# Row-tiled, paired gram matmuls and 78-row turns in a recommendation tower on Trainium2

## The reference

```python
def _cin_layer(X0, Xi, W, b):
    Wr = W.reshape(H, F0_, Fi)
    return jnp.einsum('hjk,bjd,bkd->bhd', Wr, X0, Xi) + b[None, :, None]
e = jnp.stack([tbl_0[ids[:, 0]], ..., tbl_38[ids[:, 38]]], axis=1)      # (512, 39, 16)
X0 = e; Xi = X0; res = []
for W, b in ((W0, b0), (W1, b1), (W2, b2)):
    Xi = _cin_layer(X0, Xi, W, b)
    res.append(Xi.sum(axis=2))
h = jnp.concatenate([jnp.concatenate(res, axis=1), dense_ctx], axis=1)
h = jnp.maximum(h @ W_top1 + b_top1, 0.0)
h = jnp.maximum(h @ W_top2 + b_top2, 0.0)
y = h @ W_top3
```

## Time and profile before

| | |
|---|---|
| three runs | 655.06, 651.89, 655.04 us |
| median | 655.04 us |
| the profiled execution, its own time | 654.38 us |
| its span | 652.5 us |
| PE busy | 617.7 us (95%) |
| DVE busy | 581.6 us (89%) |
| ACT busy | 558.5 us (86%) |
| POOL busy | 470.9 us (72%) |
| TensorE clock | 1.00 of full speed |

### The profile page before, as it was taken

How to read it: one execution, slowest core, us unless ns; L and a number is a source line. 1 busy time by engine, 2 the same in 40 slices (tenths; PEclk the granted TensorE clock), 3 DMA queues, 4 the chain that set the end, 5 groups by cost and what they waited for, 6 DMA issues and landing times.

```text
span 652.5 us, 14351 instructions
## 1 busy us (share of the span) xinstructions
PE 617.7 (95%) x2595; PEld 477.3 (73%) x2595; DVE 581.6 (89%) x1233; ACT 558.5 (86%) x1767; POOL 470.9 (72%) x442
## 2 busy tenths in 40 slices
PE   0389999999999999999999999999999999999998
PEld 0146788787878787878788787878787878876673
DVE  0549999999999999999999999999999999999980
ACT  3048899999999999999899989999999999999782
POOL 6778898979797989989798979798987656420000
DMA  7533404131222314040414132231405050000200
GB/s 228 135 78 88 125 19 126 34 105 53 79 81 49 109 21 137 9 137 17 126 32 121 39 91 67 67 91 39 120 8 149 1 150 5 12 18 1 65 1 0
DMA packets 44274, 46.16 MB, mean 71 GB/s; under 512 B 20896, under 2 KB 27264, under 8 KB 44233
## 3 DMA queue, kind: packets, MB, share of 16 engines
q1 hardware_dynamic: 38482, 43.59, 23.0%
q0 software_dynamic: 5120, 1.32, 2.4%
q10 hardware_dynamic: 631, 0.74, 0.4%
HBM read 44.30 MB, written 1.31 MB: 70 GB/s over the span
## 4 chain that ended last, share of the span: by engine, by line
PE 88%; issue 4%; DVE 4%; POOL 1%; ACT 1%; DMA 1%; DVEq 0%
PE ya L528 12%; PE ya L530 12%; PE ya L529 12%; PE yd L528 9%; PE yd L530 8%; PE yd L529 8%; PE misc L511 5%; PE acc L500 4%; PE acc L499 3%; PE acc L501 3%; PE acc L504 2%; DVE chain L651 2%; POOL emb L390 1%; PE yd L611 1%; PE yd L609 1%
## 5 line engine op out<-in xcount | busy, mean ns | idle before, releaser
L779 ACT ACTIVATE prods<-ya,x0t 128x128 f32<-128x128 f32 x1472 | 452.0, 519 | 40.8 <-PE ya L530 37.8
L651 DVE SCALAR_TENSOR_TENSOR chain<-yd,x0t,chain 128x128 f32<-128x128 f32 x768 | 218.2, 343 | 4.9 <-remote 4.0
L390 POOL DMA_INDIRECT emb<-in_tables,rows x160 | 158.4, 990 | 35.4 <-issue 24.3
L528 PE MATMUL ya<-w1h,x1h 128*128 128x512 f32 (+1 forms) x384 | 166.4, 433 | 3.2 <-ACT prods L779 2.1
L437 POOL TENSOR_TENSOR prod0l<-prod,prod0h 120x512 fp32r<-120x512 f32 x98 | 127.6, 1302 | 47.8 <-ACT prod0h L788 47.2
L529 PE MATMUL ya<-w1l,x1h 128*128 128x512 f32 (+1 forms) x384 | 147.5, 384 | 0.0
L530 PE MATMUL ya<-w1h,x1l 128*128 128x512 f32 (+1 forms) x384 | 147.2, 383 | 0.0
L305 POOL TENSOR_TENSOR prod<-tiles,x0a 120x512 f32<-120x512 f32 x105 | 137.3, 1308 | 12.5 <-issue 4.2
L666 DVE TENSOR_REDUCE x2t<-prods 128x128 f32<-128x1792 f32 x64 | 129.2, 2019 | 2.4 <-issue 0.3
L666 DVE TENSOR_REDUCE prods<-prods 128x128 f32<-128x1536 f32 x64 | 111.7, 1746 | 0.1
L528 PE MATMUL yd<-w1h,x1h 128*128 128x512 f32 x256 | 102.5, 400 | 1.9 <-DVE prods L651 1.6
(11 more groups left out here) (102 smaller groups left out, 620.9 us busy)
## 6 DMA issues: line engine op xcount, KB each, us to landing
tiles<-x_rows SPq DMA_DIRECT2D x236, 78.0 KB
x0a<-x_rows SPq DMA_DIRECT2D x45, 80.0 KB
emb<-in_tables,rows POOLq DMA_INDIRECT x160
w<-in_w SPq DMA_DIRECT2D x3, 832.0 KB, 5.6
w<-in_w SPq DMA_DIRECT2D x13, 192.0 KB
tiles<-x_rows SPq DMA_DIRECT2D x32, 42.0 KB
x<-x_rows SPq DMA_DIRECT2D x16, 78.0 KB
x<-x_rows SPq DMA_DIRECT2D x16, 77.8 KB
```

Source lines behind the costliest of these rows:

```text
L390: pool.indirect_dma_start(emb[:, c % 2, fo * D:(fo + 1) * D], None, a["tables"], bass.IndirectOffsetOnAxis(ap=rows[:, c, fo:fo + 1].bitcas ...
L528: pe.matmul(out, x1h[:, c % 2, xs], w1h[:, cols], start=True, stop=False)
L651: dve.scalar_tensor_tensor(out, product, x, run if step else b1[:, :], ALU.mult, ALU.add).then_inc(yd_used, 1)
L779: mm = act.activation(prods[:, :, slot_of(q) + i], ya[(NA * g + k) % YA][:, i * H:(i + 1) * H], ACT.Copy, scale=turned(c)[:, g * F1 + j:g ...
```

## The change

- **Gram.** Each gram matmul becomes two, on rows 0 to 63 and rows 64 to 127 of the same operands, each with 160 columns and a bank of its own. They go out for two groups at once, after (0,6) and (2,6); ACT copies the two results after blocks 7 and 8. `diag` is half as wide and has four buffers. For the second bank one of ACT's four `ya` banks is given up (`YA` = 3).
- **Turn.** `x0` has two copies of the 39 rows; both halves of the turn have 78 rows. It now turns the next chunk, after (1,1), and not the one after next, after (3,1).
- **Layout of the data.** The columns of a chunk are ordered in two halves. `x0_rows` is stored by halves, so a transfer's pieces are 1 KB where they were 2 KB, and 64 bytes in the store where they were 128.
- **Rounding.** The first product of a chunk is rounded at (3,7), not (3,4).

```diff
-XB = 3
+XB = 2
-YA, YD = 4, 2
+YA, YD = 3, 2
+DIAGS = 4
-G_AFTER, TURN_1 = 6, (0, 8)
+G_AFTER, TURN_AFTER = 6, (1, 1)
-HIGH_AFTER = {0: (3, 4), 1: (0, 0), 2: (0, 5), 3: (1, 0), 4: (1, 5), 5: (2, 0), 6: (2, 5)}
+HIGH_AFTER = {0: (3, 7), 1: (0, 0), 2: (0, 5), 3: (1, 0), 4: (1, 5), 5: (2, 0), 6: (2, 5)}
...
-        scratch = nc.dram_tensor("x0_rows", (CHUNKS, FP, COLS), F32, kind="Internal").ap()
-        acc0, misc = ps("acc0"), ps("misc")
+        scratch = nc.dram_tensor("x0_rows", (CHUNKS, 2, FP, HCOLS), F32, kind="Internal").ap()
+        acc0, pair = ps("acc0"), ps("pair", (P, 2, 512))
+        misc = pair[:, 0, :]
...
-                pe.transpose(misc[:, XB * F:GROUPS * F], by_group[0:F, XB, :], const[0:F, C_ID:C_ID + F]
+                pe.transpose(misc[:, XB * F:2 * XB * F], by_group[:, XB, :], const[0:XB * F, C_ID:C_ID + XB * F]
                              ).then_inc(x0t_done, 1)
...
-            def gram_group(n, g):
-                pe.wait_ge(sums_done, 2 * n + 2)
-                pe.wait_ge(diag_ready, n + 1)
-                wait_done(pe, g_ready, n)
-                pe.matmul(misc[:, 0:GB * F1], x2t[:, g % 2, :],
-                          diag[:, g % 2, :, :].rearrange("p b j -> p (b j)"),
-                          start=True, stop=True).then_inc(g_done, 1)
+            def gram_groups(ns):
+                pe.wait_ge(sums_done, 2 * ns[-1] + 2)
+                pe.wait_ge(diag_ready, ns[-1] + 1)
+                wait_done(pe, g_ready, ns[0])
+                for i, n in enumerate(ns):
+                    for h in range(2):
+                        half, cols = slice(h * HROWS, (h + 1) * HROWS), slice(i * HB * F1, (i + 1) * HB * F1)
+                        mm = pe.matmul(pair[:, h, cols], x2t[half, n % 2, :],
+                                       diag[half, n % DIAGS, :, :].rearrange("p b j -> p (b j)"), start=True, stop=True)
+                mm.then_inc(g_done, len(ns))
...
-                        if q == G_AFTER + 1 and (g or prev):
-                            evacuate_gram(GROUPS * c + g - 1)
+                        if q == G_AFTER + 1 and (g == 2 or g == 0 and prev):
+                            evacuate_gram(GROUPS * c + g - 2, 0)
+                        if q == G_AFTER + 2 and (g == 2 or g == 0 and prev):
+                            evacuate_gram(GROUPS * c + g - 1, 1)
```

More of the change, by code:

```diff
@@ L38 @@
 GROUPS = CB // GB
+HB = GB // 2
+HROWS = P // 2
+HCOLS = COLS // 2
 R0 = F + 1
@@ L287, in load_x0a @@
             for u in range(3):
-                engine.dma_start(x0a[u * R0:(u + 1) * R0, :], chunk_rows(x)[0:R0, :]).then_inc(x0a_in, 16)
+                engine.dma_start(in_halves(x0a[u * R0:(u + 1) * R0, :]), chunk_rows(x)[0:R0]).then_inc(x0a_in, 16)
         def load_tile(engine, x, i):
@@ L293, in load_tile @@
             for row, a, b in segments(i):
-                engine.dma_start(tiles[a:b, i % L0_TILES, :],
-                                 chunk_rows(x)[row:row + b - a, :]).then_inc(tile_in[i % L0_TILES], 16)
+                engine.dma_start(in_halves(tiles[a:b, i % L0_TILES, :]),
+                                 chunk_rows(x)[row:row + b - a]).then_inc(tile_in[i % L0_TILES], 16)
         def multiply0(engine, x, i):
@@ L306, in multiply0 @@
                                  ALU.mult).then_inc(prod0_ready, 1)
-        hid, hid2 = (acc0, ya[0], ya[1], ya[2]), (yd[1], ya[3])
+        hid, hid2 = (acc0, ya[0], ya[1], ya[2]), (yd[1], pair[:, 1, :])
         block = ctx.enter_context(nc.Block())
@@ L316, in store_x0 @@
                 sp.wait_ge(x0_ready, x + 1)
[L317 to L320, removed]
+                by_row = scratch[x, :, :, :].rearrange("h (f o) n -> (h f) (o n)", f=FI)
+                for i, cols in enumerate((slice(0, FT * HCOLS), slice(FT * HCOLS, FO * HCOLS))):
+                    sp.dma_start(by_row[:, cols].rearrange("q (p b) -> p q b", b=CB // 2),
+                                 xt[0:(cols.stop - cols.start) // (CB // 2), i, :].rearrange("p (q b) -> p q b", b=CB // 2),
                                  ).then_inc(scratch_in, 16)
@@ L412, in sum_dims_last @@
                     pool.wait_ge(z_adds, {8: 1, 4: 2, 2: 3}[count])
[L413 removed]
+                out = z[:, (CHUNKS - 1) * CB:].rearrange("p (g b) -> p g b", g=2 * GROUPS)
                 pool.tensor_tensor(out, terms[:, :, 0, :], terms[:, :, 1, :], ALU.add).then_inc(z_sums, 1)
@@ L763, in evacuate_x1, with evacuate_gram @@
                                ACT.Copy).then_inc(x1h_ready, 1)
-            def evacuate_gram(n):
+            def evacuate_gram(n, i=0):
                 act.wait_ge(g_done, n + 1)
-                act.activation(gram[:, :, bass.ds(n * GB, GB)],
-                               misc[:, 0:GB * F1].rearrange("p (b j) -> p j b", b=GB),
+                cols = slice(i * HB * F1, (i + 1) * HB * F1)
+                act.activation(gram[:, :, bass.ds(n * GB, GB)].rearrange("p j (h b) -> p j h b", h=2),
+                               pair[:, :, cols].rearrange("p h (b j) -> p j h b", b=HB),
                                ACT.Copy).then_inc(g_ready, 1)
@@ L799, in chunk @@
                             evacuate_layout(c + 2)
-                        if lay and (g, q - 2) == turn_after(prev):
-                            evacuate_x0t(c + 2)
-                        if not prev and (g, q) == (TURN_1[0], TURN_1[1] + 1):
-                            evacuate_x0t(1)
+                        if nxt and (g, q - 2) == TURN_AFTER:
+                            evacuate_x0t(c + 1)
                         if not nxt and (g, q) == (1, 2):
@@ L808, in chunk @@
                             act.activation(dense, dense_raw, ACT.Copy).then_inc(dense_high, 1)
-                        if q == G_AFTER + 1 and (g or prev):
-                            evacuate_gram(GROUPS * c + g - 1)
+                        if q == G_AFTER + 1 and (g == 2 or g == 0 and prev):
+                            evacuate_gram(GROUPS * c + g - 2, 0)
+                        if q == G_AFTER + 2 and (g == 2 or g == 0 and prev):
+                            evacuate_gram(GROUPS * c + g - 1, 1)
+                        if q == G_AFTER + 1 and g == 3 and not nxt:
+                            evacuate_gram(GROUPS * c + 2)
                         if nxt and (g, q) == (L0_AFTER[-1][0], L0_AFTER[-1][1] - 1):
@@ L867, in constants @@
     for row in range(P):
-        pack[row, C_MASK + row % GB] = 1.0
+        pack[row, C_MASK + row % HB] = 1.0
         pack[row, C_ID + row] = 1.0
```

64 lines of the change are left out of this document (33 added, 31 removed).

## The result

The changed kernel takes 660.0 us (median of 8 runs), the kernel before 655.1 beside it on the same chip: ratio 1.007, 95% interval 1.0046 to 1.0095. The forecast was 663.5, slower. The profiled execution took 659.8 us against 654.4, so the two traces differ by 5.4 us, near the 4.9 of the medians.

What follows compares the result with a forecast made beforehand. A closed loop of TensorE and VectorE waits, 35.1 us a chunk, bounds the kernel; 654.4 plus 9.5 (14 chunks), -1.0 (chunk 0), +0.2 (end), +0.4 (start) gives 663.5 us, range 649 to 672.

Steps and rivals of the forecast that it cites:

- The second loop: TensorE from block (0,3) to (3,1), then VectorE to (3,8); claimed to take over, +0.68 us a chunk.
- 5 steps of 0.135: In a gram pair, eight passes overlap in program order to five steps: 0.675 us.
- the switch: Going into the smaller row tiles and out again at each pair: 0.37 us, bounds 0 and 0.41.
- +0.68: Per chunk: two pairs and the turn for three grams, +0.70 us, less 0.02 spare at (3,1).
- TensorE bounds chunk 0: In chunk 0, TensorE's gram and turn work falls from 2.70 to 1.27 us; claimed -1.0 us.
- The start: Until chunk 0's x0 rows are in, finer transfers cost 0 to +1.5 us; taken as +0.4.
- A: Gram pairs: tiles fully side by side, switch hidden, pair 0.54 us; -4.5 us over the chunks, 649 us; chance 0.23.
- B: Gram pairs: five steps, no cost of switching, pair 0.675 us; about 653 us; chance 0.15.
- C: Gram pairs: tiles do not overlap, or each pass waits for its weights; 672 to 675 us; chance 0.15.
- D: Finer transfers: 0.2 us more an issue delays GpSimd's product, TensorE waits at (0,3); 8 us more; chance 0.05.
- the 2 us of room: GpSimd's first product in a chunk may come 2 us later before it hurts; 13 issues precede it.
- Edits at nothing: Three ScalarE banks, later rounding, smaller diagonal, gram copies and finer steady transfers were all costed at nothing.

Runs made afterwards that it cites:

- turn_back: Changed kernel with the 78-row turn back after block (3,1), turning two chunks ahead: 651.2 us against 649.7 for the kernel before, chunk period 35.22 us.
- before_turn78: Kernel before with only the turn's second transpose reading 78 rows instead of 39, place unchanged: 648.8 us against 649.7, chunk period 35.11 us.
- single_tiles: Changed kernel with one row-tiled gram at a time after (0,6), (1,6), (2,6), (3,6), turn back behind (3,1): 660.3 us against 655.1 for the kernel before, ratio 1.0059.
- before_ya3: Kernel before with only ScalarE's blocks going round three PSUM banks instead of four: 650.0 us against 649.7.
- round_3_4: Changed kernel with the rounding of the first product back after (3,4) from (3,7): 660.5 us against 655.1 for the kernel before.
- full_rows: Changed kernel with 128-row, 320-column grams instead of row tiles, same places, scores wrong: 659.4 us against 649.7 for the kernel before, ratio 1.0140.
- full_3_0: Changed kernel with full 128-row grams, two each after (3,4) and (0,1), turn after (3,1), scores wrong: 657.0 us against 650.2 for the kernel before.

## Why the prediction came out as it did

**The mechanism held.** The second loop took over at (3,1), VectorE waits there where it did not, 0.28 us and not the 0.7 expected, the gap at (0,3) grew to about 1, and the period rose. turn_back and before_turn78 show it twice: 0.24 to 0.31 us of work on the same engine counts in one place and not in the other.

**The pair was mis-sized.** I put 5 steps of 0.135 and 0.37 for the switch, 1.05; it is 4 steps and 0.40, 0.946 (1.08 from its first pass to the next block's second matmul, where I expected 1.3). The argument for five was the program's order of passes; the trace has the passes go out in couples from the first on. The way in and out, taken from one 39-row transpose, was right within 0.03, and single_tiles has it again. The Trainium skill's rule in "TensorEngine Tiling (Array Packing)", Key Properties, that a change of the tiling mode drains the engine, agrees with both. Its figure of about 4 ns of issue overhead for each further tile ("TensorE: Matmul & The Clock Gate", Measured speedup vs the span model) stands against 7 ns between the two starts here: the tiles overlap as that page has them.

**The chunk.** Predicted +0.68, measured +0.34. TensorE's stretch grew by 2 x 0.946 + 0.235 - 3 x 0.549 = 0.48 where I had 0.70; most of that is the pairs, 0.21. A loss of 0.07 at the gram of (0,6) in the kernel before, whose weights came late there, went with it and was not in my sum; VectorE's stretch and its distance behind TensorE gave back 0.06, of which I had 0.02. 0.48 - 0.07 - 0.06 is 0.35.

**The rest.** Between the starts of chunks 1 and 15 the traces differ by 5.1 us (I had 9.5). Chunk 0: predicted -1.0, measured +0.2, 39.1 to 39.3 us. The work did get less, but TensorE does not bound that chunk: VectorE and ScalarE stop in it for some 4 us in both kernels. So the step "TensorE bounds chunk 0" failed, and its -1.0 hid a little of the surplus in the chunks. The profile mostly names "remote" for it (waits of 36 to 60 us, kernel before, then after):

```profile
DVE chain L651 <- remote: 4.0, 1, 4.0
```

```profile
DVE chain L657 <- remote: 4.6, 1, 4.6
...
ACT prods L790 <- remote: 4.4, 1, 4.4
```

After it TensorE's granted clock was lower for a while in the trace of the changed kernel and not in that of the one before. The windows of 44 to 46 us (TensorE busy 0.77 of 2 us, and 0.43 in the next) and 48 to 50, kernel after:

```profile
44.00:46.00 2.00, 0.77 (x4) 0.31 (x2) 0.00 (x0) 0.00 (x0) 0.94 (x1) 1.00 0.51 136
...
48.00:50.00 2.00, 2.00 (x7) 1.33 (x6) 2.00 (x4) 2.00 (x10) 1.69 (x3) 0.59 0.55 163
```

0.59 is a mixture of 1.2 and 2.4 GHz. This does not belong to the change: on the chip of single_tiles the kernel before had a mean granted clock of 1.00 in 4 of 18 launches (653.9 us in the median), 0.997 in 9 (655.1) and 0.995 in 5 (656.3). The launches with a lower clock are 1 to 2.5 us longer; the 5.1 us lie in chunks at 1.00 in both traces. In the studies where the kernel before took 655 us, chunk 0 of the profiled kernels lasted 38.8 to 42.7 us, in those where it took 650 only 34.5 to 36.7: most of the 5 us between chips is here. What stops the two engines is open; no kernel was made for it. The start (-0.15, I had +0.4), chunk 15 (+0.24, I had nothing) and what follows it with the last gram (+0.05, I had +0.2) are small. -0.15 + 0.2 + 5.1 + 0.24 + 0.05 is 5.4.

**Rivals.** A is wrong in its sum by the 0.40 of the switch, though its half on the overlap was right. B is wrong by the same 0.40 and has a step too many. C has no overlap, and there is full overlap. D: the 14.75 us of the earlier trace rows is one of the longer chunks. In the median over the chunks the 28 tile transfers issue in 13.7 us before and in 14.6 after, 0.03 more an issue and not 0.2, so 13 of them stay well under the 2 us of room. The queue's smaller packets (70291 in all against 44274) take the same 23.0% of the DMA engines. In the steady part GpSimd waits for tiles twice, 4.2 us together (once, 3.4, before), and TensorE's period shows neither. No kernel has the finer transfers alone.

**Edits at nothing.** Banks and rounding are shown to cost nothing here (before_ya3, round_3_4), the latter only under cover of the wait at (0,3). The gram copies and the smaller diagonal were not tried alone; the sum leaves no room for them.

## What to carry to other kernels

Where two engines wait for each other, write down each closed loop through the banks they share, one for each place where either waits or has little to spare, not the busiest engine's sum. Price an edit by the loops whose stretch it stands in, and before moving work out of one, read how much the next place has to spare (0.30 us at (0,8) decided half of the gain here), and which shared bank the moved work will meet. The sum of a loop proves nothing by itself, for any round trip gives the period: look for the one whose handovers wait and in whose stretches neither engine waits for the other. A mode of an engine that pays a fixed price to enter wants its work gathered, in a place that no loop counts.

## What the runs showed of the hardware

- Two float32 matmuls on rows 0 to 63 and 64 to 127 ran in step: their passes go out in couples 7 ns apart, 0.136 us a couple at 160 columns (kernel after). A full gram's two passes of 320 columns start 0.27 apart.
- Going into such tiles and out costs 0.40 us whether 4 passes stand between or 8 (0.672 and 0.946 us in all; single_tiles, kernel after); the weights of the first pass and of the matmul behind the last are not loaded ahead.
- A full gram whose weights are not loaded ahead takes 0.36 to 0.37 us in its first pass in place of 0.27 (full_rows at (0,6), full_3_0 at (3,4)).
- A transpose with 39 rows pays 0.31 us of the same kind (0.54 us for a turn with it, 0.235 without; before_turn78 has 0.31 in the same place).
- 59% more DMA packets for 3% fewer bytes (44.90 MB against 46.16, tiles in pieces of half the size) left the main queue's share of the DMA engines at 23.0%; 28 issues took 14.6 us in place of 13.7.
